# Loading whole experts straight into their ring slots, one ahead, in a routed block on one core

## The reference, cut to what matters

```python
xt = x.reshape(B * S, H)                                   # 2048 x 512
sh_mid = gelu(einsum('th,ehd->ted', xt, Wsh_up))           # 2 shared experts, d = 256
shared_out = einsum('ted,edh->th', sh_mid, Wsh_down)
probs = softmax(xt @ W_router)                             # 16 routed experts
top_v, top_i = top_k(probs, 2)
gate = sum(one_hot(top_i, 16) * top_v[..., None], axis=1)
rt_mid = gelu(einsum('th,ehd->ted', xt, Wrt_up))
routed_out = einsum('ted,edh->th', rt_mid * gate[:, :, None], Wrt_down)
out = x + gb * (shared_out + routed_out)
```

## Time and profile before

| | |
|---|---|
| three runs | 965.27, 969.03, 970.52 us; median 969.03 |
| the profiled execution | 969.45 us, span 967.7 us |
| granted TensorE clock, mean | 0.974 of full speed |
| busy share of the span | PE 93%, DVE 56%, POOL 41%, ACT 40% |

### The profile page before, as it was taken

The page is one execution under the profiler, slowest core; times in us unless marked ns, Lnnn a source line. Parts: engine busy times, 40 slices in busy tenths (PEclk is TensorE's granted clock), DMA queues, the critical chain, the costliest instruction groups (busy, mean ns, idle before and its releaser), DMA issues.

```text
span 967.7 us, 13687 instructions
## 1 busy us (share of the span) xinstructions
PE 896.3 (93%) x4264; PEld 722.9 (75%) x4265; DVE 537.9 (56%) x983; ACT 383.8 (40%) x632; POOL 399.2 (41%) x314
## 2 busy tenths in 40 slices
PE   7898879999998999999999899989997999989993
PEld 2457658878776788887888788878876888878782
DVE  5896998987657111355144514451772444444488
ACT  2566455573735542321232122225441333333441
POOL 2322200100022437236104600469337989889273
PEclk9898979999998999999999999999999999999997
DMA  9549477566054536144115301564545777786686
GB/s 358 181 132 278 143 226 253 163 197 205 1 186 146 168 99 202 49 157 148 44 54 172 122 33 55 191 226 159 164 144 152 231 239 232 236 264 201 210 262 206
DMA packets 106720, 166.69 MB, mean 172 GB/s; under 512 B 8344, under 2 KB 53400, under 8 KB 105136
## 3 DMA queue, kind: packets, MB, share of 16 engines
q1 hardware_dynamic: 59184, 112.07, 34.4%
q0 software_dynamic: 10336, 35.13, 11.5%
q10 hardware_dynamic: 37152, 18.88, 6.6%
HBM read 98.63 MB, written 67.42 MB: 172 GB/s over the span
## 4 chain that ended last, share of the span: by engine, by line
PE 60%; POOL 14%; DVE 13%; issue 5%; DMA 4%; ACT 3%; POOLq 1%; SPq 0%; DVEq 0%; ACTq 0%
PE kv_ps L419 6%; PE kv_ps L421 6%; PE kv_ps L420 6%; PE kk_ps L419 6%; PE kk_ps L421 6%; PE kk_ps L420 6%; POOL ex_w L2444 5%; PE mm_ps L419 4%; PE mm_ps L420 4%; PE mm_ps L421 4%; POOL ex_w L2442 4%; DVE raw_ps L1352 2%; PE up_ps L419 2%; PE mm_ps L860 1%; DVE mix L1358 1%
## 5 line engine op out<-in xcount | busy, mean ns | idle before, releaser
L1552 DVE TENSOR_TENSOR silu<-kk_ps,silu 128x512 fp32r<-128x512 f32 x64 | 44.3, 692 | 205.2 <-ACT silu L2155 204.9
L2151 ACT ACTIVATE kk_ps<-kk_ps 128x512 f32<-128x512 f32 x64 | 37.2, 582 | 210.4 <-PE kk_ps L421 210.3
L419 PE MATMUL kk_ps<-xk,cm_w 128*128 128x512 f32 x256 | 101.0, 394 | 0.4 <-DVE silu L1552 0.4
L419 PE MATMUL kv_ps<-cm_w,silu 128*128 128x512 f32 x256 | 100.6, 393 | 0.0
L421 PE MATMUL kk_ps<-xk,cm_w 128*128 128x512 f32 x256 | 99.8, 390 | 0.0
L421 PE MATMUL kv_ps<-cm_w,silu 128*128 128x512 f32 x256 | 99.7, 390 | 0.0
L420 PE MATMUL kk_ps<-xk,cm_w 128*128 128x512 f32 x256 | 99.7, 389 | 0.0
L420 PE MATMUL kv_ps<-cm_w,silu 128*128 128x512 f32 x256 | 99.6, 389 | 0.0
L2327 POOL TENSOR_TENSOR rs<-mv,neghalf 128x4 f32<-128x4 f32 x12 | 13.6, 1133 | 162.7 <-DVE mv L1281 162.6
L1841 DVE TENSOR_TENSOR xsT<-xs_ps,xsT 128x512 fp32r<-128x512 f32 x42 | 29.1, 692 | 90.9 <-ACT xsT L2236 90.9
L2320 POOL TENSOR_TENSOR cm_w<-stage,cm_w 128x1024 fp32r<-128x1024 f32 x16 | 38.7, 2425 | 91.8 <-ACT cm_w L1942 91.8
(11 more groups left out here) (275 smaller groups left out, 2368.4 us busy)
## 6 DMA issues: line engine op xcount, KB each, us to landing
xs_s<-zero ACTq DMA_DIRECT2D x13, 1024.0 KB, 6.0
stage<-in_wex POOLq DMA_DIRECT2D x24, 512.0 KB, 5.0
xsb<-xs_s SPq DMA_DIRECT2D x44, 256.0 KB, 3.5
ys_s<-ysb SPq DMA_DIRECT2D x41, 256.0 KB, 2.8
stage<-in_wcm SPq DMA_DIRECT2D x16, 512.0 KB, 3.8
wmod<-in_wmod SPq DMA_DIRECT2D x6, 1024.0 KB, 11.7
ex_raw<-in_wex SPq DMA_DIRECT2D x6, 1024.0 KB, 7.5
stage<-in_wtm SPq DMA_DIRECT2D x10, 512.0 KB, 6.2
```

Of the source, the lines that this page charges most:

```text
L419: pe.matmul(out, lhs[0], rhs[0], start=first, stop=False)
L1552: dve.tensor_tensor(silu[:, g % NSILU, 1, :], kk_ps[g % 2][:, :], silu[:, g % NSILU, 0, :].bitcast(F32), ALU.subtract).then_inc(s_silo, 1)
L2151: act.activation(kk_ps[g % 2][:, :], kk_ps[g % 2][:, :], ACT.Silu).then_inc(s_silu, 1)
```

## The change

- Expert e (4 to 15) is loaded whole, 1 MB in one DMA, into the lo half of its own ring slot (`raw_of`), and split there with two instructions of 2048 elements per partition: hi from raw, lo over raw. A new overlay raw6 names slot 6 for it.
- The load of expert e must wait until its slot is free, since it goes into the slot itself: s_up 8 for expert 4, `expert_done(e - 5)` and a small operation on thr for the others.
- Expert 5 is loaded only after `last_ht_load`. From there the load of e + 1 is issued in front of the split of e.
- The four loads of gb follow the split of expert 12; before they stood between its halves.
- On PE `table_row` moves between the halves of `shared_up(1)`; before it stood in front of the last quarter of the first tile of `shared_down(1)`.
- The count that `gathered` expects of the semaphores of the expert loads is halved, as there are half as many loads.

The base adds stay where they were on Pool. VectorE's and SP's lists are unchanged.

```diff
-            before = 32 * NB if i < TT else 0 if i < TT + 2 else 16 * (NE - PRE)
+            before = 32 * NB if i < TT else 0 if i < TT + 2 else 16 * (NE - PRE) // 2
...
-            shared_up(1)
-            shared_down(1, [0], first)
+            shared_up(1, [0, 1])
             table_row()
-            shared_down(1, [0], rest)
+            shared_up(1, [2, 3])
+            shared_down(1, [0], every)
             shared_down(1, [1], every)
...
+            def raw_of(e):
+                return ex_raw[:, ring_slot(e), 1] if ring_slot(e) < BASE + PRE else raw6[:, 1]
+
+            def expert_load(e):
+                if e < ERING:
+                    pool.wait_ge(s_up, SB * KT)
+                else:
+                    expert_done(e - ERING)
+                    pool.tensor_tensor(thr[:, e:e + 1], zero[:, 0:1], zero[:, 1:2], ALU.add)
+                pool.dma_start(raw_of(e), wex_d[2 + e]).then_inc(s_exs[e % 2], 16)
+
+            def expert_split(e):
+                pool.wait_ge(s_exs[e % 2], 16 * ((e - PRE) // 2 + 1))
+                hi, lo = (ex_w[:, ring_slot(e), i] for i in range(2))
+                n = 2 * (e - PRE)
+                pool.tensor_tensor(hi, raw_of(e), zero[:, 0:1].to_broadcast([P, UNIT]), ALU.add).then_inc(s_exd, 1)
+                pool.wait_ge(s_exd, n + 1)
+                pool.tensor_tensor(lo, raw_of(e), hi.bitcast(F32), ALU.subtract).then_inc(s_exd, 1)
+                pool.wait_ge(s_exd, n + 2)
+                pool.sem_inc(s_exr, 8)
...
-            halves = 2 * (NE - PRE)
+            expert_load(PRE)
             pool.wait_ge(s_wlo, 38)
-            expert_load(0)
-            expert_load(1)
             pool.sem_inc(s_exr, 8 * PRE)
             pool.wait_ge(s_tab, 1)
-
-            for n in range(halves):
-                expert_split(n)
-                if n + 2 < halves:
-                    expert_load(n + 2)
-                if n == 1:
...
+            expert_split(PRE)
+            for t in range(2, SB * TT):
+                x4_load(t)
+            ht_lo(2)
+            for t in range(SB * TT):
+                base_add(t)
+            last_ht_load()
+            expert_load(PRE + 1)
+
+            for e in range(PRE + 1, NE):
+                if e + 1 < NE:
+                    expert_load(e + 1)
+                expert_split(e)
+                if e == PRE + TT * 2:
                     pool.wait_ge(s_gates, 1)
```

More of the change, by code:

```diff
@@ L183, in adaln_block @@
         ht1 = sbuf(overlay, "ht1", [P, 2, KT, T], F32R)
+        overlay.close()
+        overlay = ExitStack()
+        sbuf(overlay, "ex_w_head6r", [P, RING - 1, 2, UNIT], F32R)
+        raw6 = sbuf(overlay, "raw6", [P, 2, UNIT])
         overlay.close()
@@ L2415, in _ @@
             weight_lo(37)
[L2417 to L2425, removed]
             def expert_done(e):
```

## The result

| | before | changed |
|---|---|---|
| 20 executions each, median | 965.54 us | 969.13 us |
| lowest to highest | 963.89 to 970.52 | 965.73 to 975.57 |
| profiled execution, span | 967.7 us | 964.0 us |
| mean granted clock, profiled execution | 0.974 | 0.977 |

The ratio is 1.0036, interval 1.0023 to 1.0049: the change makes the kernel 3.5 us slower, less than the 0.5% that the prediction set as its bound, and with 20 executions each still more than none. It is inside the range and on the wrong side of the forecast, which was 1.3 us faster. The median before is 965.54 with 20 executions, not the 969.03 of three from which the forecast started.

A forecast was written before the change was run, and what follows sets the result against it. PE, busy 93%, bounds the kernel; a faster Pool is worth at most PE's 2.34 us wait at tile 32. PE leaves the loop 1.3 us earlier: 969.45 - 1.3 = 968.1 us profiled, 967.7 by the median; range 964.8 to 973.3.

The forecast's parts named there:

- the one on gathered tiles: Routed loop: a gathered load beside a whole expert lands in 6.4 us, 0.5 inside the 6.9 limit.
- up to 2 us late: At 769 to 780, 3 MB in flight: a tile may be this late; before tile 32, 1.4 us costs nothing.
- Rival C: Routed loop: every whole expert load makes a gathered tile late; at 0.8 us each +7.5 us, 976.5; chance 0.12.
- The 2.34 us at tile 32: PE's wait for Pool's split of expert 13, taken as the whole worth of a faster Pool.
- The first tile: Start of routed loop: PE's 3.06 us wait belongs to table, scatters and gathered load; at most 0.37 us sooner.
- The table: table_row between shared_up(1)'s halves: small products covered by PE's 1.81 us wait; tab 0.37 us sooner, 0 as other end.
- Pool's steps: Pool in routed stage: split 8.41 us, period 10.20 instead of 10.85, expert 13 ready at 869.1.
- the chances beyond 0.5% slower, 0.04 and 0.12: Whole kernel: 0.04 from a grown wait for Pool, 0.12 from late gathered tiles; stated together as slower 0.15.

The follow-up runs named there:

- b_mask: Kernel before with one more register operation per tile on PE, awaiting the same number: 1.0000 (0.9983 to 1.0017) of the kernel before.
- b_table_moved: Kernel before with b_mask's extra operation and table_row moved as in the change: 1.0012 (0.9991 to 1.0033) of the kernel before.
- a_mask: Changed kernel with only b_mask's extra register operation per tile on PE: 1.0053 (1.0032 to 1.0074) of the kernel before.
- a_load5_early: a_mask with expert 5's load issued in front of the base adds instead of after last_ht_load: 1.0035 (1.0012 to 1.0058) of the kernel before.
- a_mid_late: a_mask with the four mid loads in front of the last split instead of behind the base adds: 1.0042 (1.0019 to 1.0064) of the kernel before.
- a_gb_late: a_mask with the four gb loads moved behind the last split: 1.0059 (1.0036 to 1.0082) of the kernel before.
- a_l5_mid: a_mask with expert 5 loaded before the base adds and the mid loads in front of the last split: 0.9999 (0.9981 to 1.0018) of the kernel before.
- a_quiet: a_mask with table_row's old order, expert 5 earlier, mid before and gb behind the last split: 1.0004 (0.9988 to 1.0020) of the kernel before.
- a_quiet_tab: a_quiet with table_row where the change puts it: 1.0005 (0.9994 to 1.0016) of the kernel before.
- a_table_back: a_mask with PE's old order of table_row: 1.0026 (1.0003 to 1.0049) of the kernel before.
- a_halves: a_mask with each expert loaded by two DMAs of 512 KB, rows of 4 KB, into the same slot: 1.0054 (1.0031 to 1.0077) of the kernel before.

## Why the prediction was wrong, point by point

- **The step that failed** is the one on gathered tiles. It put a gathered load beside a whole expert at 6.4 us, 0.5 inside the limit, and in the loop that holds: 6.0 at most in the changed kernel's trace where, of Pool's loads, only an expert's is in flight. (The row it took the 6.4 from had half an expert under way beside the megabyte of gb: that load was issued at 851.97 and landed at 857.58.) It saw the 3 MB at 769 to 780, wrote "up to 2 us late" (measured 2.12), and then let 1.4 of that cost nothing, because PE would otherwise wait for expert 13, and left the rest out of the sum. In the trace expert 13 was ready 2.6 us before PE's transpose of tile 32, so all of the wait counted. It did not follow its own list to the second place: the four gb loads with expert 14 behind them are 2 MB, the gathered load lands in 8.3, and PE stands 1.13 us. Rival C had every whole load make a tile late; in the changed kernel's trace only two of them do, where other bulk loads are in flight too. Together the two waits are 3.25 us, more than the 2.34 that the change was to take away.
- **The gain was read from one execution.** The 2.34 us at tile 32 were the worth of the whole change, in an execution that took 969.45 us, 3.9 over the median of 20. b_mask's execution had no such wait, b_table_moved's had 3.08 us. The forecast took a wait that varies as fixed, and gave no place to the chance that it is not there.
- **The clock was left out.** Waits of 2 to 3.5 us on PE were costed at their length. In a_mask each of three of them had 3.4 us at half clock behind it, about 1.5 us more apiece. Pauses of this length are in every kernel's trace; which of them brings the clock down differs from execution to execution, and before's profiled execution had no fall where b_mask's had one. Over the 20 executions of the changed kernel the mean clock runs from 0.967 to 0.977, and the three over 973 us have the three lowest (0.967 to 0.969). An estimate of its part: in a_mask, a_load5_early, a_mid_late and a_gb_late, 41 executions, the mean clock is 0.0014 (give or take 0.0009) under that of the kernel before in the same jobs, and 0.0014 of 966 us is 1.3 us, out of a mean loss of 4.6. In a_l5_mid, a_quiet and a_quiet_tab, 37 executions, that difference is 0.0000.
- **The first tile** is a wait that the prediction gave to table, scatters and gathered load, and expected to shrink by 0.37. It is set by what stands in front: with expert 4's load issued 0.3 us ahead of the first gathered one the wait was 3.4 us in a_mask, a_load5_early and a_mid_late, 1.18 in the changed kernel's own trace (where tab, and with it the gathered load, came 1.8 us later); with the load behind the tile it went to 0.4. In before two halves stood there, for 3.06 us, so this is not a cost of the whole load.
- **The table:** the copy to tab was forecast 0.37 us sooner. It ended 0.5 us sooner in b_table_moved and a_mask, and 1.3 us later in the profiled changed kernel, where the clock fell at shared_up(1). With the old order and such a fall it is 16.0 us (b_mask) and 16.3 us (a_quiet) after the first scatter, against 15.8 in the changed kernel, so like with like the move brings tab 0.2 to 0.5 us sooner. That the small products are covered was right. Whether the move is worth anything in the kernel's time the runs don't tell: level in a_quiet_tab, while a_table_back has half of a_mask's loss.
- **Pool's steps were right,** and this is the part that the trace of before could carry: split of 2048 at 8.41 (measured 8.28), period 10.20 (10.07), expert 4's data 7 us after issue (5.0), expert 5's at 7.1 (7.8), expert 13 ready 152.7 us after the first scatter (150.1), tile 32 without a wait for Pool over 2.3 us. A slip without effect: the chances beyond 0.5% slower, 0.04 and 0.12, make 0.16 and not 0.15.

**What stays open.** Whether expert 5's load and mid simply add up, or each hides behind the other: by the ratios they gave 1.8 and 1.1 us against a_mask and together 5.4, each within some 3 us, which holds both. Pool's readiness at tile 32 doesn't explain it in the traces at hand, for in a_mask, a_load5_early and a_mid_late PE doesn't wait for Pool there; but these are single executions. The split of the loss, 1.3 us of clock and the rest waits, is an estimate with an interval of 0.9 us either way. Whether 8 KB rows hold up the gathered loads more than 4 KB rows do is open too.

## What to carry to other kernels

When a load is made larger or moved, list for each place what else will be in flight in those few microseconds, on every queue, and compare the time to landing of the small, urgent loads with their deadline there. One megabyte beside them was harmless in the loop here, two and three were often not; and what counted was what had been issued in front of them, an urgent load issued just ahead of a bulk one was not held up. Two bulk transfers that nobody needs soon (mid, gb) belong where no urgent one is under way; moving one of them and the load it met gave back the whole loss. A wait that a single profile shows is a sample: before building a gain on it, look at a second execution.

## What the runs showed of the hardware

- A gathered load of 256 KB took 2.5 us to land at the least. In the changed kernel's loop it took up to 6.0 us beside 1 MB of a Pool load, 8.3 beside 2 MB and 9.2 beside 3 MB; in other traces 6.5 beside 1 MB (a_table_back, issued at 867.89), 7.8 to 9.3 beside 2 MB (a_table_back, a_mask). Beside the eight bsb loads at the end of the changed kernel's loop it was 6.6. SP issues the gathered loads and the stores of the tiles, Pool the rest.
- The order of issue decides. In the changed kernel's trace the seven gathered loads of the loop that had a Pool load only behind them, issued less than 2.5 us after, landed in 2.5 to 2.8 us; the seven issued while a single expert's load had been under way for 0.8 us or more, and had 2.5 us or more to go, landed 0.6 to 1.4 us after that load. The Trainium skill (DMA: Bandwidth & Descriptors, Queues, rings and completion order) has each engine take turns between queues at packet granularity. The trace shows more than turns: which load was issued first counted too. Whether the size of the rows has a part no run tells; with rows of 4 KB (a_halves) the slowest took 7.2 and 8.5 us.
- After pauses of 1.6 to 3.5 us in PE's work the granted clock was half for 3.4 us in some executions and full in others: full after 1.81 us in the profiled kernel before and half after 1.80 us in b_mask, which have the same program up to there; full after 3.06 us before, half after 3.42 us in a_mask.
- Pool's tensor_tensor scales as two sizes said it would: 1.25 us at 512, 2.39 at 1024 (before), 4.60 at 2048 elements (changed). The 4497 ns that the Trainium skill gives for 2048 (GPSIMD Engine Reference, 3.1 Elementwise — side-by-side cycle accounting) is 0.1 under the measured one.
